# Selective scan on GpSimd: the sum of a half state moved one step back, the drive one step closer

## What is computed

```python
def step(state, inp):
    d, b, c, u = inp
    dA = jnp.exp(d[..., None] * A)
    state = state * dA + (d * u)[..., None] * b[:, None, :]
    y = jnp.einsum('bdn,bn->bd', state, c)
    return (state, y)
```

## Time and profile before

| | |
|---|---|
| Median of 3 runs | 1647.42 us (1647.31 to 1654.25) |
| Time of the profiled execution | 1645.0 us |
| Its span | 1642.5 us |
| Busy in the span | PE 87%, DVE 79%, POOL 75%, ACT 64% |
| Mean granted clock of PE | 0.937 |

### The profile page before, as it was taken

One profiled execution on the slowest core, in us unless ns is written; L12 is line 12 of the kernel. 1 busy time (PEld: TensorE's weight loads), 2 busy tenths in 40 slices (PEclk: granted clock), 3 DMA queues, 4 the chain that ended last, 5 costly groups with the idle time before them and its releaser, 6 DMA issues.

```text
span 1642.5 us, 23259 instructions
## 1 busy us (share of the span) xinstructions
PE 1427.5 (87%) x7632; PEld 1143.5 (70%) x7632; DVE 1300.6 (79%) x2375; ACT 1043.6 (64%) x2407; POOL 1234.8 (75%) x613
## 2 busy tenths in 40 slices
PE   4646789999999999999999999987477999898996
PEld 1213568878878878878888788875256676676784
DVE  3897688899888899888899889886637668487575
ACT  3886366666666666656667666664447657577474
POOL 1345189999989999989999899999667347166263
PEclk9766799999999999999999999999699999998998
DMA  4466513425623434633453632325342022121021
GB/s 166 165 231 210 184 61 123 141 84 154 200 81 126 134 113 139 195 113 102 126 151 129 178 115 77 120 77 160 98 149 76 27 97 76 42 83 64 27 71 58
DMA packets 121664, 194.03 MB, mean 118 GB/s; under 512 B 10740, under 2 KB 60408, under 8 KB 120008
## 3 DMA queue, kind: packets, MB, share of 16 engines
q1 hardware_dynamic: 120392, 188.36, 35.0%
q0 software_dynamic: 1152, 4.19, 1.5%
HBM read 145.99 MB, written 46.53 MB: 117 GB/s over the span
## 4 chain that ended last, share of the span: by engine, by line
PE 39%; DVE 22%; POOL 15%; issue 12%; ACT 8%; DMA 2%; SPq 1%; POOLq 0%; DVEq 0%; ACTq 0%
PE banks L595 9%; PE banks L596 8%; PE banks L597 8%; POOL act_buf L1925 5%; DVE state L1148 5%; POOL state L1265 3%; POOL state L1242 3%; PE banks L1467 2%; PE banks L1468 2%; PE banks L1469 2%; DVE banks L445 2%; DVE banks L1983 1%; DVE w_lo L1051 1%; DVE negmax L1088 1%; PE banks L803 1%
## 5 line engine op out<-in xcount | busy, mean ns | idle before, releaser
L1265 POOL TENSOR_TENSOR state<-state,Cn 128x1024 f32<-128x1024 f32 x120 | 293.2, 2444 | 28.5 <-DVE state L1148 28.1
L1148 DVE TENSOR_TENSOR_SCAN state<-banks,state 128x512 f32<-128x512 f32 x256 | 310.6, 1213 | 4.6 <-ACT banks L969 2.4
L1242 POOL TENSOR_TENSOR state<-dtu_sb,Bn 128x1024 f32<-128x1024 f32 x128 | 313.8, 2452 | 0.1
L1925 POOL TENSOR_TENSOR act_buf<-act_buf,wb 128x512 f32<-128x512 f32 x128 | 165.5, 1294 | 171.8 <-ACT act_buf L1825 171.6
L1270 POOL TENSOR_TENSOR y_sb<-y_sb,state 128x1024 f32<-128x1024 f32 x120 | 287.4, 2395 | 9.4
L969 ACT ACTIVATE banks<-dt_sb,negA 128x512 f32<-128x512 f32 x256 | 177.4, 693 | 104.4 <-DVE state L1148 103.8
L595 PE MATMUL banks<-x_hi,w_hi 128*128 128x512 f32 (+1 forms) x512 | 186.6, 365 | 27.1 <-DVE qT_lo L1078 15.6
L597 PE MATMUL banks<-x_hi,w_lo 128*128 128x512 f32 (+1 forms) x512 | 178.4, 348 | 0.0
L596 PE MATMUL banks<-x_lo,w_hi 128*128 128x512 f32 (+1 forms) x512 | 178.1, 348 | 0.0
L1973 DVE TENSOR_TENSOR hid_lo<-banks,hid_hi 128x512 fp32r<-128x512 f32 x136 | 93.7, 689 | 53.6 <-ACT hid_hi L1837 51.5
L1983 DVE TENSOR_TENSOR banks<-banks,act_buf 128x512 f32<-128x512 f32 x136 | 94.4, 694 | 51.5 <-POOL act_buf L1925 27.7
(11 more groups left out here) (219 smaller groups left out, 4449.6 us busy)
## 6 DMA issues: line engine op xcount, KB each, us to landing
Cn<-scratch_bc SPq DMA_DIRECT2D x64, 256.0 KB, 3.4
x_hi<-scratch_xs SPq DMA_DIRECT2D x32, 512.0 KB, 4.6
x_lo<-scratch_xs SPq DMA_DIRECT2D x32, 512.0 KB, 6.2
Bn<-scratch_bc SPq DMA_DIRECT2D x64, 256.0 KB, 3.8
scratch_acc<-acc_sb SPq DMA_DIRECT2D x64, 256.0 KB, 2.1
wb<-scratch_wT SPq DMA_DIRECT2D x64, 256.0 KB, 3.2
acc_sb<-scratch_acc SPq DMA_DIRECT2D x48, 256.0 KB, 3.0
w_stage<-in_w SPq DMA_DIRECT2D x32, 256.0 KB, 3.6
```

Of the source, the lines that this page charges most:

```text
L1148: nc.vector.tensor_tensor_scan(row, dA[:, :], row, 0.0, ALU.mult, ALU.add) \
L1242: nc.gpsimd.tensor_tensor(st[:, k % 4], dtu[:, 2 * h:2 * h + 2, :], Bn[:, state % NB, :].unsqueeze(1).broadcast_to([P, 2, T]), ALU.mult).t ...
L1265: nc.gpsimd.tensor_tensor(to, st[:, k % 4], Cn[:, state % NB, :].unsqueeze(1).broadcast_to([P, 2, T]), ALU.mult).then_inc(S["gated"], 1)
L1925: nc.gpsimd.tensor_tensor(act_[:, N % 3, :], act_[:, N % 3, :], wb[:, E % 3, :], ALU.mult) \
```

## The change

The sum leaves its place behind its own product and stands behind the product of the step after; the drive of a step is that of two half states ahead, no longer three. In step k POOL does product k, sum k - 1, drive k + 2. For the last state of a batch sum k stands in its own step still, with the DMA behind it and now ahead of the drive. The four buffers of `st` stay, as does each wait's target.

```diff
+        def accumulate(k):
+
+            h = k % 2
+            pool.wait_ge(S["gated"], k + 1)
+            nc.gpsimd.tensor_tensor(y[:, 2 * h:2 * h + 2, :], y[:, 2 * h:2 * h + 2, :],
+                                    st[:, k % 4], ALU.add).then_inc(S["piece_done"], 1)
+
         for k in range(NDRIVE):
             state, h = divmod(k, 2)
             b, r = divmod(state, NS)
@@
             nc.gpsimd.tensor_tensor(to, st[:, k % 4],
                                     Cn[:, state % NB, :].unsqueeze(1).broadcast_to([P, 2, T]),
                                     ALU.mult).then_inc(S["gated"], 1)
-            if r > 0:
-                pool.wait_ge(S["gated"], k + 1)
-                nc.gpsimd.tensor_tensor(y[:, 2 * h:2 * h + 2, :], y[:, 2 * h:2 * h + 2, :],
-                                        st[:, k % 4], ALU.add).then_inc(S["piece_done"], 1)
-            if k + 3 < NDRIVE:
-                drive(k + 3)
+            if k >= 1 and 0 < (k - 1) // 2 % NS < NS - 1:
+                accumulate(k - 1)
             if r == NS - 1:
-
+                accumulate(k)
                 pool.wait_ge(S["piece_done"], added(k))
                 nc.gpsimd.dma_start(d["y"][b][:, 2 * h * T:2 * (h + 1) * T], half(y, h), accum_op=ALU.add) \
                     .then_inc(S[f"y_added{h}"], 16)
+            if 3 <= k + 2 < NDRIVE:
+                drive(k + 2)
```

## The result

| | before | after |
|---|---|---|
| Median (runs) | 1647.31 us (5: 1643.14 to 1654.25) | 1659.38 us (5: 1654.93 to 1663.2) |
| Ratio after / before | | 1.0068, 95% interval 1.0043 to 1.0093 |
| Profiled execution, its span | 1645.0, 1642.5 us | 1663.2, 1661.2 us |
| Start of product 127 (POOL) | 1140.02 us | 1159.91 us |

The change makes the kernel slower, by 12.1 us in the medians. The profiled execution of after is the slowest of its five, 3.8 us above their median; the same kernel measured again (first experiment) gave 1657.36 us, 10.4 above before, and a profile of 1656.0 us. So the loss is 10 to 12 us, and the profile shown here has several us more than that; the second profile is put beside it wherever a size matters.

A forecast was written before the change was run, and what follows sets the result against it. PE, with DVE where late, paces the stage; POOL only from product 106. Changes of batch 8.4 plus end 2.5 make 10.9 us, added to 1647.4: 1658 us, range 1646 to 1667 (8 in 10).

The forecast's parts named there:

- The saving, 0.12 us a sum, and only behind product 106: POOL's sums lose the wait for their own product, 0.12 us each, worth something only where POOL is the end.
- The end, +2.5: End of the stage: one postponed sum and drive, 4.7 us, less savings, put POOL's last DMA 2.5 us later.
- cover of 5 us: End of the stage: PE's last product is done 5 us ahead of DVE's statistics, so late scan 254 costs nothing.
- The changes of batch, 2.8 each, 8.4: Three changes of batch: late drive 33 delays scan 66 by 4.2 us, 1.4 covered; 2.8 reach PE, 8.4 together.
- They are not won back: After each change of batch: the 2.8 us PE loses stay lost, as DVE works at one stretch into the splits.
- that gap moves as a whole: PE's 3.52 us wait for weight splits at 463.06, behind the change of batch, shifts later without shrinking.
- In between, nothing: Elsewhere scans wait up to about 1 us for drives, costed at nothing; 5 us more if each were passed on.
- The splits, plus or minus 3, left out of the sum: Weight splits on DVE meet POOL's moved boundaries: one can lose 2 us or gain 1; plus or minus 3 us, not summed.
- signs to look for: Sums 2.35 us behind products, over 30 scan waits totalling over 20 us, later L826 and scan 254, product 106 near 1001.6.
- a cover deep enough at the changes: Rival: at changes of batch PE does other work while heads are late, only the tail counts; 1650 us, chance 0.33.
- every wait passed on: Rival: throughout the stage each scan's delay reaches the end, about 20 us in all; 1667 us, chance 0.12.
- a sum that keeps its delay: Rival: the operation, not the wait, makes the sum's 0.12 us, so POOL is later at each place; 1662 us, chance 0.06.
- a POOL that paces the stage: Rival: POOL bounds the whole stage, so 0.12 us a step saves 14 us from the start; 1633 us, chance 0.04.

The follow-up runs named there:

- first experiment: The changed kernel measured once more with no edit: 1657.36 us, ratio 1.0048 to before.
- odd columns: Before and after, each with weight splits of groups 1 to 3 as one-input zero writes over 127 of 128 or 511 of 512 columns: 1646.61 and 1658.36 us.
- the two experiments with one input: Weight splits in before and after replaced by one-input zero writes: even columns 1637.13 and 1648.50 us, odd columns 1646.61 and 1658.36 us.

## Why the prediction was right, step by step

The forecast was 1658 us, slower by over 0.5%; 1659.38 and, again, 1657.36 were measured. The sum of 10.9 us lies between the 10.4 and 12.1 of the two pairs of medians. The two causes that were summed, the late drive at the changes of batch and the work postponed to the end, hold; that the total fits so closely is in part luck. In the second profile the splits added 5.2 us that the sum did not have, while the changes cost 2.6 less than forecast and the start gained 2.2. For the profiled execution 1655.9 was forecast: the first took 1663.2, the second 1656.0.

- **The saving, 0.12 us a sum, and only behind product 106.** Right. Starts stand 2.35 us apart instead of 2.47, product 114 starts 56.9 us behind product 106 as against 57.5, and the order that takes the wait away without moving a drive or a sum by a step gains 1.95 us over those 21 steps (the step put it at 0.64 + 1.6 = 2.2). With this order in the whole stage no more than these 2.0 are gained.
- **The end, +2.5.** Right: 2.3 in both profiles of after. The parts are measured too: 4.5 of the 4.7 us of postponed work show in the run that goes back to the old order. Scan 254 was 5 us later than the rest, as forecast, and the cover of 5 us was used up to 0.25 us, closer than I had argued.
- **The changes of batch, 2.8 each, 8.4.** The mechanism is right, and shown by putting the drive ahead of the last sum and DMA: the cost goes. Product 30 to 32 was forecast at 18.9 and took 19.0. L826 moved by 3.4 at the first change of batch, for which 2.8 was forecast. Over the three it came to 9.0 and 5.8 us, against 8.4. "They are not won back" and "that gap moves as a whole" were wrong: PE's gap of 3.52 us shrank to 1.34, and at the first change 2.3 us come back from block 17 to 18 in both profiles. With odd columns all of it came back (block 15 at 4.28 us, 17 at 7.17, 18 at 4.26).
- **In between, nothing.** Right away from splits and changes: from block 18 to 25, 34 to 41 and 50 to 60 the distance is level, with scans waiting.
- **The splits, plus or minus 3, left out of the sum.** This is the term that was mis-sized. Both profiles of after lose there, 8.8 and 5.2 us, and the run with only the drive closer 11.0. I had taken the effect for luck with either sign, one lost boundary against one gained. The sign is no luck: every kernel with the splits of before and another order in this part of the stage loses (after and five more). A part of the size is, 1.8 us in each stretch in which L1062 starts just behind an operation of POOL.
- **Not forecast at all**: between blocks 1 and 5 the two profiles of after gain 1.2 and 1.9 us, where a pair of output-weight splits fell differently between POOL's operations (below). This is in the -2.2 at block 9, which is why 2.3 + 5.8 + 5.2 makes 11.1 and not 13.3.
- The *signs to look for* held in the main: 27 scan waits (over 30 forecast; 32 in the second profile), 37.8 us (over 20). Product 106 came at 1010.73 in this profile, forecast 1001.6, and at 1001.96 in the second, in which the distance of product 127, 11.1, is that of the forecast.
- *The rivals*: a cover deep enough at the changes is ruled out by the 3.4 us of L826, every wait passed on by the level stretches, a sum that keeps its delay by the 2.35 us, and a POOL that paces the stage by the order product, drive, sum, which takes away the waits and saves nothing ahead of product 106.

How the two causes at the splits divide is open in part. For the ports: the order product, drive, sum loses about 1.5 us in each stretch with no scan that waits for POOL, single splits change from 0.68 to 2.4 to 2.9 us (below), and L1062 makes 1.8 us of difference between stretches of one kernel. For late drives: the kernels with a closer drive lose 0.7 to 6.5 us more than that order, and the later sum alone loses only 1.9. Of these, after again and the old order from step 100, with L1062 short throughout, stand at 0.7 to 0.8; after's first profile has 4.3, of which 3.5 go with L1062; most of the 6.5, with the drive closer only, stays unexplained. Against either as the whole: in a stretch of splits only two or three scans of after wait, of 0.67 to 1.25 us each, and the stretches with three such waits lose less (1.7 to 1.8) than those with two (3.5); and the splits themselves, 24 of them in before and then in after, have hardly grown (38.4 us in all in before, 40.6 in after and 37.9 in after again):

```profile
L1051 DVE SCALAR_TENSOR_TENSOR w_lo<-w_stage,w_hi x24: 680/1598/2814, 340.1 to 879.2; 128x512 fp32r<-128x512 f32 x24
```
```profile
L1051 DVE SCALAR_TENSOR_TENSOR w_lo<-w_stage,w_hi x24: 681/1600/2890, 340.0 to 892.6; 128x512 fp32r<-128x512 f32 x24
```

Other ones of them are long, and it would have to matter which. An experiment in which splits touch nothing that POOL's operations need was not found; two tries shared it still.

The two best versions are before's own order with the drive ahead of the sum, from step 100 (0.9990) or throughout (0.9996). Neither can be told from before by its ratio.

## What to carry to other kernels

A wait between two operations of one engine has a small price, here 0.12 to 0.18 us, and counts only where that engine is the end; how far an operation stands ahead of the engine that consumes it can be worth 3 us at one place. So, if the gap is to be filled at all, fill it with an independent operation that is already near (product, drive, sum; here it gained 2 us at the end and nothing that the ratio can show), rather than by postponing one and drawing its neighbour closer, and look first at places where the engine has its extra work (here the last state of a batch, with a sum and a DMA). Where work is postponed past the last wait of an engine, add it to the end in full.

## What the runs showed of the hardware

**A weight split of DVE and an operation of POOL take turns, and microseconds hang on who starts first.** The same split, its third operation of a group, on DVE, with POOL's at the same time. In before:

```profile
354.13 0.68 DVE L1051 SCALAR_TENSOR_TENSOR w_lo<-w_stage,w_hi 128x512 fp32r<-128x512 f32 x1
```
```profile
354.21 2.85 POOL L1242 TENSOR_TENSOR state<-dtu_sb,Bn 128x1024 f32<-128x1024 f32 x1
```

In after:

```profile
353.77 2.46 DVE L1051 SCALAR_TENSOR_TENSOR w_lo<-w_stage,w_hi 128x512 fp32r<-128x512 f32 x1
```
```profile
353.28 2.39 POOL L1242 TENSOR_TENSOR state<-dtu_sb,Bn 128x1024 f32<-128x1024 f32 x1
355.64 2.83 POOL L1272 TENSOR_TENSOR state<-state,Cn 128x1024 f32<-128x1024 f32 x1
```

The split that starts 0.08 us ahead of a drive takes 0.68 us, and the drive 2.85 instead of 2.40. The one that starts 0.49 us behind a drive ends 0.59 us after POOL's next start, and that next operation is the long one. DVE gets its turn at the boundary though POOL leaves no gap. What changes the time is therefore half a microsecond of phase, 1.8 us at a time; at L1062 (above) 0.03 us of phase made 2.3 us of duration, for 256 numbers. The same split took 2.43 us in after again, 2.56 with the drive closer only, 2.44 with the drive first at the last state and 2.92 with product, drive, sum; it took 0.68 with the sum later only, with the new order from step 100 and in before again. The Trainium skill, SBUF — State Buffer, section Who interferes with whom, has the lock go to the instruction that issues first; the rows agree, with DVE's turn at the next boundary.

**It was not only the form with two SBUF inputs.** The rows of the two experiments with one input show it, 0.42 to 2.58 us and 0.74 to 2.85.

**The pair of output splits that the start gains by** took 3.16 us in before and 1.42 in after, the same effect to the change's advantage:

```profile
219.27 3.16 DVE L1056 SCALAR_TENSOR_TENSOR ow_lo<-w_stage,subln,ow_hi 128x512 fp32r<-128x512 f32 x2 [0.93 <-ACT ow_hi L881]
```
```profile
220.48 1.42 DVE L1056 SCALAR_TENSOR_TENSOR ow_lo<-w_stage,subln,ow_hi 128x512 fp32r<-128x512 f32 x2 [0.92 <-ACT ow_hi L881]
```

**A wait for an operation just ahead on the same engine**: 2.47 instead of 2.35 us from start to start for a sum behind its product, 2.53 for a drive behind its sum. A DMA that waits for its own sum stands 2.70 us behind it (1136.71 to 1139.41), where the sum alone takes 2.36.
